# Edges of layers 1 and 3: GpSimd waits for two products at once and issues eight gathers behind the wait

## What is computed

```python
# layer 1
g = descriptors @ Wdesc.T                       # 64 numbers an edge -> 128
xj_all = ssp(xa @ Wj.T + bj)
pxj = g * xj_all[idx_j]                         # the gather, and the product
xj = jax.ops.segment_sum(pxj, idx_i, num_segments=x.shape[0])

# layer 3
W = ssp(edge_attr @ mlp_w1.T + mlp_b1) @ mlp_w2.T + mlp_b2   # 50 numbers an edge -> 128
W = W * C[:, None]
messages = W * (x[j] @ lin1_w.T)                # the gather, and the product
agg = jax.ops.segment_sum(messages, i, num_segments=x.shape[0])
```

## Time and profile before

| | us |
|---|---|
| median of 3 runs | 8407.85 |
| lowest and highest run | 8391.69, 8443.28 |
| span of the profiled execution | 8429.8 |
| gathers of layer 1, from the first to the last start | 3839.8 to 5164.8 |
| gathers of layer 2 | 5530.1 to 6812.0 |
| gathers of layer 3 | 6966.1 to 8326.5 |
| busy: PE, DVE, ACT, POOL | 4817.4, 4456.8, 2631.9, 4200.4 |

### The profile page before, as it was taken

The page is one execution under the profiler, slowest core; times in us unless marked ns, Lnnn a source line. Parts: engine busy times, 40 slices in busy tenths (PEclk is TensorE's granted clock), DMA queues, the critical chain, the costliest instruction groups (busy, mean ns, idle before and its releaser), DMA issues. The chain is left out here.

```text
span 8429.8 us, 124318 instructions
## 1 busy us (share of the span) xinstructions
PE 4817.4 (57%) x25123; PEld 3687.3 (44%) x25124; DVE 4456.8 (53%) x14435; ACT 2631.9 (31%) x7317; POOL 4200.4 (50%) x4981
## 2 busy tenths in 40 slices
PE   7766666603344444754455456656666656677676
PEld 6444454402333333643444444344444444455455
DVE  7555555533333334673333335856666674555556
ACT  2333344302222223661000002733333343333333
POOL 0355555536666665344555552046666625555552
PEclk9667667655555556775555667878777766777767
DMA  1333333255111113522222221022222212222221
GB/s 53 99 102 104 102 108 108 89 47 49 43 41 43 42 42 83 127 70 60 57 58 58 56 58 33 5 61 64 63 64 63 64 32 59 51 54 52 51 52 42
DMA packets 833939, 528.65 MB, mean 63 GB/s; under 512 B 588596, under 2 KB 741000, under 8 KB 833416
## 3 DMA queue, kind: packets, MB, share of 16 engines
q1 hardware_dynamic: 702152, 261.57, 14.1%
q0 software_dynamic: 131648, 265.56, 11.4%
HBM read 399.11 MB, written 127.68 MB: 62 GB/s over the span
## 5 line engine op out<-in xcount | busy, mean ns | idle before, releaser
L1367 POOL DMA_INDIRECT l2e_rows<-l_rows,columns x832 | 794.2, 955 | 852.9 <-POOLq L226 364.3
L834 POOL DMA_INDIRECT src_records<-sort_rec,sort_idx x784 | 764.1, 975 | 735.3 <-DVEq L727 477.1
L1367 POOL DMA_INDIRECT spare<-l_rows,k_dst_of x784 | 742.7, 947 | 771.9 <-DVE l3e_prod L2412 373.7
L1233 POOL DMA_INDIRECT dst_rows<-l0d_out,l0d_idx x832 | 842.3, 1012 | 492.2 <-issue 238.1
L1367 POOL DMA_INDIRECT table<-l_rows,k_dst_of x784 | 742.2, 947 | 641.4 <-DVE l1e_prod L1605 310.7
L887 DVE TENSOR_TENSOR spare<-spare,l1e_pR 128x128 f32 x832 | 238.5, 287 | 848.0 <-DMA l0m_rows<-dst_rows 712.5
L1192 PE MATMUL l0d_pX<-table,l0d_ohT 128*128 x1664 | 432.5, 435 | 401.4 <-ACT l0d_ohT L1210 265.5
L1575 PE MATMUL l1e_pG<-k_weights,table 64*128 64x128 f32 x1568 | 222.5, 429 | 669.8 <-ACT table L1596 414.3
L2245 PE MATMUL l2e_pR<-l2e_z,l2e_oh 128*128 128x128 f32 x1664 | 309.7, 345 | 476.2 <-DVE both L887 405.0
L2345 PE MATMUL l3e_pH<-table,k_weights 50*128 50x256 f32 x784 | 358.7, 548 | 372.2 <-DMA run_ml<-both 348.8
L1192 PEld LDWEIGHTS l0d_pX<-table,l0d_ohT 128*128 128x128 f32 x1664 | 369.3, 308 | 452.2 <-issue 452.2
(11 more groups left out here) (417 smaller groups left out, 13358.6 us busy)
## 6 DMA issues: line engine op xcount, KB each, us to landing
l0m_rows<-dst_rows SPq DMA_DIRECT2D x196, 264.0 KB, 2.8
sort_rows<-lo_rows SPq DMA_DIRECT2D x196, 256.0 KB
sort_rec<-rec SPq DMA_DIRECT2D x98, 472.0 KB
l2e_lrow<-dst_local SPq DMA_DIRECT2D x208, 128.0 KB
table<-src_records SPq DMA_DIRECT2D x196, 128.0 KB
table<-src_records SPq DMA_DIRECT2D x196, 100.0 KB
dst_rows<-l0d_out,l0d_idx POOLq DMA_INDIRECT x832
l2e_rows<-l_rows,columns POOLq DMA_INDIRECT x832
```

The lines of the kernel that those rows point to most:

```text
L834: e.indirect_dma_start(kn.by_src_rec[:, :], bass.IndirectOffsetOnAxis(ap=r["idx"][:, st.quad, j:j + 1], axis=0), r["rec"][:, st.quad, j, : ...
L1233: e.indirect_dma_start(kn.by_dst[:, :], bass.IndirectOffsetOnAxis(ap=r["idx"][:, st.quad, j:j + 1], axis=0), r["out"][:, st.quad, j, :], N ...
L1367: e.indirect_dma_start(r["rows"][:, i % ring, j, 0:width], None, table[:, :], bass.IndirectOffsetOnAxis(ap=columns[:, i * G + j:i * G + j ...
```

## The change

GpSimd's waits are taken for `burst` steps at a time, where `burst` is a quarter of the ring: 2 steps in layers 1 and 3, 1 step in layer 2. Ahead of an even step i it waits until i-6 products are done and then issues the gathers of steps i and i+1. The last step is bounded by `min(..., steps)`.

```diff
 def gather_rows(kn, e, r, table, width, columns, used, ring=4, steps=STEPS):
 
+    burst = ring // 4
     for i in range(steps):
-        if i >= ring:
-            e.wait_ge(used, i - ring + 1)
-        take_waits(e, kn.tally)
+        if i % burst == 0:
+            if i >= ring:
+                e.wait_ge(used, min(i - ring + burst, steps))
+            take_waits(e, kn.tally)
         for j in range(G):
             e.indirect_dma_start(r["rows"][:, i % ring, j, 0:width], None, table[:, :],
```

## The result

| | before | after |
|---|---|---|
| median, us | 8425.57 | 8670.22 |
| lowest, highest | 8391.69, 8459.17 | 8651.45, 8704.27 |
| runs | 4 | 4 |
| span of the profiled execution | 8429.8 | 8702.5 |

The recorded ratio is 1.0312, with a 95% interval from 1.0263 to 1.0362: the change makes this kernel slower by 3.1%. (Such ratios and intervals are quoted from the record; the quotient of two medians can differ a little, and is 1.029 here.) The prediction was 8448 us with a range up to 8570, so the result lies outside it. Lines of the kernel after are two further down from L1369 on (the gathers; L1367 before), so the products are L1607 (layer 1) and L2414 (layer 3), the transposes L1566 and ScalarE's copy L1598.

A forecast was written before the change was run, and what follows sets the result against it. Layers 1 and 3 were taken as bound by gathers and arithmetic coupled, TensorE's results being told late during gather runs. 31 + 19 - 10 = +40 us on the median of 8407.85 gave 8448 us, range 8290 to 8570.

The forecast's parts named there:

- What bounds the stages: Layers 1 and 3: neither gathers nor arithmetic alone; while gathers run, TensorE's results are told late, 5.2 us in one case.
- The rule that spoke against it all: Trainium skill page: engine and DMA ports cannot contend, so grouping gathers couldn't touch TensorE; change worth 0 us.
- What it removes, and the lead, at nothing: Layers 1 and 3: 94 of 188 waits removed per stage gain nothing; gathers at most one product later are hidden.
- Openings, -10 us: Opening runs of gathers shorten from 44 to 40 in layer 1 and 36 to 32 in layer 3; together -10 us.
- Layer 1, +31 us: Layer 1's long stretch goes from 6.83 to 7.0 us a step over 184 steps: +31 us, bounds -153 and +105.
- I take 28.3 us: Layer 1: assumed length of a cycle of sixteen gathers, 7.1 us a step, between 25.7 and 29.7 us.
- the tenth of the steps that I left in cycles of eight at 6.0 us: Layer 1: some 10% of steps should stay in cycles of eight gathers at 6.0 us, making the mean 7.0.
- the point of decision at 10.0 us: Layer 1: a run's second product done after its eighth gather, 10.0 us in, gives a stop and the short cycle.
- Layer 3, +19 us: Layer 3: fours become eights, at 7.1 for 7.00 us a step over 186 steps: +19 us, bounds -74 and +56.
- Rival 2: Long runs lock in: layer 1 all sixteens, +105; layer 3 +56; openings -10; total 8559 us; chance 0.27.
- Rival 1: Short cycles of eight lock in: layer 1 -153, layer 3 down to -74, openings -10; 8170 to 8290 us; chance 0.20.
- Rival 3: Nothing moves: gather time plus what must happen without gathers sets the total; 8400 to 8410 us; chance 0.15.

The follow-up runs named there:

- e8: Kernel before with only the first ring of gathers in layers 1 and 3, later products not waiting for rows; 7063.45 us, a single run.
- e13: The changed kernel again, no edit, on a second-kind chip where the kernel before took 6755.12 us; 6754.36 us, 0.9995.
- e4: Kernel before plus a wait, after every second step of layers 1 and 3, until that step's gathers landed; first-kind chip, 8148.95 us, 0.972.
- e5: Kernel before plus a wait, after every third step (12 gathers) of layers 1 and 3, until these gathers landed; 8386.4 us, 1.0031.
- e7: Kernel before with rows of layers 1 and 3 brought by plain transfers on SyncE's queue, GpSimd idle in both loops; 7006.94 us, a single run.
- e3: Kernel before, still waiting at every step, but for one product more (i-6 for i-7) in layers 1 and 3; 8387.2 us, 0.9994.
- e16: Kernel before plus a landing wait after every 8 gathers in layers 1 and 3, on a second-kind chip; 7177.24 us, 1.0617.

## Why the prediction was wrong

**What bounds the stages: right.** Neither the gathers nor the arithmetic alone: e8 shows 2.92 us a step without gathers and e13 5.0 with gathers and without late updates; both together took 6.83. That the late copies go with runs of gathers is shown by e4, e5, e7 and e8, and 13.4 us of lateness in a run of sixteen stands beside the 5.2 of the earlier trace rows. The rule that spoke against it all, by which the change would be worth 0 us, didn't give the outcome.

**What it removes, and the lead, at nothing: right** (e3, 0.9994). **Openings, -10 us: right** (59.7 for 64.5 us and 48.5 for 54.2 us, runs of 40 and 32). The numbers of stops, about 50 and 80, were right too (47 and 85).

**Layer 1, +31 us: the mechanism right, the size wrong; it was +120.** The step that failed is "I take 28.3 us" for a cycle of sixteen, between 25.7 (a product slips into the run) and 29.7 (none does). It is 30.2 us, the upper end and half a microsecond over it; over the stretch, counted as above, 46 cycles of sixteen take 30.0 us on average. The cycle of 27.50 us, by which I chose the middle, had a rest of 1.7 us after its first gather, and was no cycle of sixteen without a rest. Five of the 46 cycles have such a rest, and take 25.6 to 30.0 us; the 41 others all take 30.0 to 30.4.

The second failing step is the tenth of the steps that I left in cycles of eight at 6.0 us. There is none now. Mostly the product that closes a run of eight is early enough (at 8.4 us: 4398.58 + 0.69 - 4390.89). But the point of decision at 10.0 us was wrong too. In twelve of the 41 cycles this product was a little late, and GpSimd paused 0.70 to 0.90 us after the eighth gather where it pauses 0.30 elsewhere; it then issued eight more and rested 10 us, and the cycle took 30.2 to 30.4 us all the same:

```profile
4360.63 0.94 POOL L1369 DMA_INDIRECT table<-l_rows,k_dst_of  x1 [10.04 <-DVE l1e_prod L1607]
...
4371.19 0.94 POOL L1369 DMA_INDIRECT table<-l_rows,k_dst_of  x1 [0.70 <-issue]
...
4390.89 0.94 POOL L1369 DMA_INDIRECT table<-l_rows,k_dst_of  x1 [10.02 <-DVE l1e_prod L1607]
```

A stop as such doesn't give the short cycle: the five short cycles that the kernel before has in layer 1 had rests of 2.3 us.

**Layer 3, +19 us: this is the larger miss; it was +164.** The price of 7.1 us a step for cycles of eight was the mean of a mixture, where eights follow fours. Three in a row gave 43.9 us, 7.3 us a step, and I took that for the upper bound. But the rows say more: from 7254.32 to 7285.02 the first two take 30.7 us, 7.7 us a step, and only the third, with 13.2 us, pulls the mean down. After the change the cycle of 16.05 us is the common one, 8.0 us a step: 43 of 75 eights take 16.0 us or more, where 7 of 43 did. I costed the missing fours with a mean in which they stood: before, an eight behind a four took 12.9 us on average (9 of them), and one behind another eight 14.1 (17 of them). But that is not all, for behind another eight it takes 15.5 us now, and no run shows why.

"The change leaves these kinds alone" failed for the sixteens as well. The cycle of 28.20 us, 7.05 us a step, was no run of sixteen at a stretch: GpSimd paused twice in it, 1.41 and 0.69 us.

```profile
7046.05 0.95 POOL L1367 DMA_INDIRECT spare<-l_rows,k_dst_of  x1 [1.93 <-DVE l3e_prod L2412]
...
7052.16 0.95 POOL L1367 DMA_INDIRECT spare<-l_rows,k_dst_of  x1 [1.41 <-issue]
...
7062.57 0.94 POOL L1367 DMA_INDIRECT spare<-l_rows,k_dst_of  x1 [0.69 <-issue]
```

The nine sixteens of the kernel after take 33.6 us, which is (8.4 - 7.0) x 36 = 50 of the 164 us; the eights, at 7.7 us a step, make the rest.

**Rivals.** Rival 2, long runs lock in, was the one that came, with layer 1 as priced (+105, measured +120) and layer 3 three times as dear (+56, measured +164); its 8559 us are 111 short mostly for that reason. Its doubt, the more so as the clock might rise in longer rests, came to nothing: 0.61 for 0.59 in layer 1's stretch. Rival 1, short cycles lock in, didn't come from this change. e4 forces such cycles and takes 8149 us, just under the 8170 to 8290 given for it, but not with the parts priced: by the traces layer 1 is 151 us shorter (-153) and layer 3 128 us (-74 at most). Rival 3, nothing moves, is what happens on the second kind of chip, though for another reason.

**How the numbers followed.** The sum was put near the middle of bounds whose upper ends, 105 + 56 - 10, were each a pattern by itself and not the edge of a spread. In layer 1 the change forces one pattern on every cycle (46 of 46), so the choice was between patterns, and the means of a mixture should have had less weight. For the total even the upper ends fell short (8559), since layer 3's was itself such a mean.

## What to carry to other kernels

Where a stage is a cycle of runs and rests, a change that fixes the length of the run must be priced by what that run does when it follows itself, not by its mean in a mixture; and even that price came out too low here (14.1 us for an eight behind an eight before, 15.5 after). Look whether the results of other engines are told late during a run of indirect gathers; if so, a rest after eight can be worth more than the waits that are saved (-2.8% against +3.1% here), and grouping the waits is the wrong way. Such a tuning holds for the chip on which it was made: the same rest was -2.8% on one chip and +6.2% on another, so measure on several before it is kept. Across both, the kernel before is the safer of the three.

## What the runs showed that I had not expected

**The same program takes 20% less time in some groups of runs.** 8366 to 8426 us on the chips of the one kind, 6752 to 6759 on those of the other, with the same duration of a gather (944 to 947 ns). The kernel before was not profiled on the second kind; e13, which takes the same time there, stands for it. Other phases with indirect transfers gain as well: GpSimd's idle time ahead of the gathers of L834 falls from 735.3 to 312.8 us and ahead of L1233 from 492.2 to 272.0:

```profile
L834 POOL DMA_INDIRECT src_records<-sort_rec,sort_idx x784 | 764.1, 975 | 735.3 <-DVEq L727 477.1
```

```profile
L834 POOL DMA_INDIRECT src_records<-sort_rec,sort_idx x784 | 780.9, 996 | 312.8 <-issue 229.3
```

(The first row is of before on the first kind, the second of e13.) Why the kinds differ isn't shown by any run here, and neither is that it is the chip and not the time at which a group ran.

**A stop that nothing explains.** GpSimd rests 1.67 us after some gathers, in layer 1 of the kernel after behind those of 4013.84, 4180.21, 4511.83, 4843.56 and 5173.79: once after 88 gathers and then every 176. e13's run of 784 gathers has none, but e16, on the same second kind and with a rest after every eight, has eight of them in layer 1. Its cause stays open.

```profile
4180.21 0.94 POOL L1369 DMA_INDIRECT table<-l_rows,k_dst_of  x1 [10.54 <-DVE l1e_prod L1607]
4182.82 0.94 POOL L1369 DMA_INDIRECT table<-l_rows,k_dst_of  x1 [1.67 <-issue]
```
